# GpSimd's map additions moved behind the next image's statistics, and a later wait for the last special columns

## The reference

```python
def _gn(v, G=32, eps=1e-05):             # group norm, 12 channels a group
    g = v.reshape(B, H, W, G, C // G)
    m, s = mean and var of g over (1, 2, 4)
    return ((g - m) / sqrt(s + eps)).reshape(v.shape)

def conv(x, w1, b1, w2, b2, bias_w, bias_b):
    bias = x @ bias_w.T + bias_b
    xf = rfftn(x.reshape(B, H, W, 4, 96), axes=(1, 2), norm='ortho')
    xr, xi = xf.real, xf.imag            # below: einsum('...bd,bdk->...bk')
    r1 = relu(xr * w1[0] - xi * w1[1] + b1[0])
    i1 = relu(xr * w1[1] + xi * w1[0] + b1[1])
    r2 = r1 * w2[0] - i1 * w2[1] + b2[0]
    i2 = r2 * w2[1] + i1 * w2[0] + b2[1]
    return irfftn(complex(r2, i2), s=(H, W), norm='ortho') + bias

out = x + conv(_gn(x), ...)
```

## Time and profile before

| | us |
|---|---|
| median of three executions | 462.18 (461.31 to 462.39) |
| the profiled execution | 459.74 |
| its span in the profile | 457.6 |
| PE busy | 400.7 |
| DVE busy | 344.6 |
| ACT busy | 227.7 |
| POOL busy | 66.5 |

### The profile page before, as it was taken

The page is one execution under the profiler, slowest core; times in us unless marked ns, Lnnn a source line. Parts: engine busy times, 40 slices in busy tenths (PEclk is TensorE's granted clock), DMA queues, the critical chain, the costliest instruction groups (busy, mean ns, idle before and its releaser), DMA issues.

```text
span 457.6 us, 19262 instructions
## 1 busy us (share of the span) xinstructions
PE 400.7 (88%) x8530; PEld 355.4 (78%) x8530; DVE 344.6 (75%) x768; ACT 227.7 (50%) x504; POOL 66.5 (15%) x72
## 2 busy tenths in 40 slices
PE   4529778899899998999899998999899998995896
PEld 4418667787788988988788988988788887984794
DVE  3676988887797788868688788768787778769324
ACT  2632765326644476427643566437642575435320
POOL 0000007600060005100150006000240007000000
PEclk9758999999999999999999999999999999998899
DMA  6770000053001700052001700151002600130003
GB/s 212 212 210 0 4 1 4 2 184 130 3 5 36 278 4 4 26 178 112 4 4 50 265 4 4 35 208 73 5 3 94 221 3 4 37 140 1 4 4 138
DMA packets 12566, 33.22 MB, mean 73 GB/s; under 512 B 4994, under 2 KB 6692, under 8 KB 12484
## 3 DMA queue, kind: packets, MB, share of 16 engines
q1 hardware_dynamic: 12484, 32.00, 20.1%
HBM read 16.26 MB, written 12.58 MB: 63 GB/s over the span
## 4 chain that ended last, share of the span: by engine, by line
PE 62%; DVE 22%; issue 4%; SPq 4%; ACT 4%; DMA 2%; DVEq 0%
PE bank L552 62%; DVE r L1066 2%; DMA bias_all<-in_bias_b 2%; DVE rsum L1059 2%; DVE xs L1006 2%; DVE xs L1008 2%; DVE z L991 2%; DVE xs L1004 1%; DVE dev L1022 1%; DVE dev L1024 1%; SPq L511 1%; DVE sX L1020 1%; SPq L506 1%; DVE rho L991 1%; DVE g L1073 1%
## 5 line engine op out<-in xcount | busy, mean ns | idle before, releaser
L552 PE MATMUL bank<-biasw,y 128*64 128x384 f16 x1152 | 112.5, 339 | 4.5 <-DVE g L1073 4.4
L552 PEld LDWEIGHTS bank<-biasw,y 128*64 128x64 f16 x1152 | 94.2, 196 | 7.8 <-issue 5.2
L552 PE MATMUL bank<-w2s,rho 128*64 128x96 f16 x3072 | 83.9, 208 | 0.2 <-issue 0.2
L552 PEld LDWEIGHTS bank<-w2s,rho 128*64 128x64 f16 x3072 | 80.8, 109 | 3.6 <-issue 2.8
L907 ACT ACTIVATE z<-bank 128x384 f16<-128x384 f32 x72 | 35.2, 489 | 65.7 <-PE bank L552 65.0
L552 PE MATMUL bank<-w1R,y 128*128 128x192 f16 (+3 forms) x768 | 59.6, 228 | 1.6 <-issue 1.1
L552 PE MATMUL bank<-tab,x_sb 128*128 128x128 f32 x384 | 52.5, 290 | 9.6 <-DMA x_sb<-in_x 5.8
L991 DVE SCALAR_TENSOR_TENSOR z<-bank,z 128x384 f16<-128x384 f32 x72 | 40.0, 557 | 26.3 <-ACT z L907 25.9
L552 PEld LDWEIGHTS bank<-tab,x_sb 128*128 128x128 f32 x384 | 48.2, 201 | 14.3 <-issue 8.0
L892 ACT ACTIVATE g<-bank 128x384 f16<-128x384 f32 x64 | 31.0, 484 | 55.8 <-PE bank L552 55.7
L991 DVE SCALAR_TENSOR_TENSOR rho<-bank,rho 128x256 f16<-128x256 f32 (+2 forms) x128 | 40.1, 364 | 23.8 <-ACT rho L925 15.4
(11 more groups left out here) (104 smaller groups left out, 464.4 us busy)
## 6 DMA issues: line engine op xcount, KB each, us to landing
x_sb<-in_x SPq DMA_DIRECT2D x16, 768.0 KB, 6.8
out<-o_sb SPq DMA_DIRECT2D x14, 768.0 KB, 3.5
y<-y SPq DMA_DIRECT2D x24, 128.0 KB, 2.8
out<-o_sb SPq DMA_DIRECT2D x8, 192.0 KB, 1.9
tab<-in_tab SPq DMA_DIRECT2D x1, 672.0 KB, 5.8
o_sb<-in_bias_wt SPq DMA_DIRECT2D x4, 144.0 KB, 2.8
b1s<-in_b1h SPq DMA_DIRECT2D x1, 384.0 KB, 5.0
tab<-in_tab SPq DMA_DIRECT2D x1, 291.5 KB, 2.7
```

Source lines behind the costliest of these rows:

```text
L552: return nc.tensor.matmul(o, lhsT, rhs, start=start, stop=stop, **kw)
```

## The change

Three things are changed. The third bias product of `p4` stands before j = 7 and no longer before j = 6. The `gi` loop is entered when seven of eight banks of `rho` are evacuated; the wait for the eighth stands in `c2_rho` of gi = 0, between half 0 and half 1. GpSimd waits for all 23 steps of the statistics of image b + 1 (for the last image: those of image 7 again) and then does the map additions of image b itself.

```diff
@@ p4 @@
                 for j in range(8):
-                    if j in (2, 4, 6):
-                        gi = j // 2 - 1
+                    if j in (2, 4, 7):
+                        gi = {2: 0, 4: 1, 7: 2}[j]
                         if more:
                             c2_bias(b, p, gi, more, first)
                         elif gi:
@@ c2_rho @@
                 for half in range(2):
+                    if gi == 0 and half == 1:
+                        pe.wait_ge(rhoh_ready, 8 * b + 8)
+                        pe.wait_ge(rhol_ready, 8 * b + 8)
                     for slot, tile, k in ((0, 0, 0), (1, 1, 0), (2, 1, 1), (3, 2, 1)):
@@ image, on PE @@
                 p4(b, p, more, first)
-                pe.wait_ge(rhoh_ready, 8 * b + 8)
-                pe.wait_ge(rhol_ready, 8 * b + 8)
+                pe.wait_ge(rhoh_ready, 8 * b + 7)
+                pe.wait_ge(rhol_ready, 8 * b + 7)
                 for gi in range(8):
@@ GpSimd @@
             for b in range(BATCHES):
-                pool.wait_ge(rhol_ready, 8 * b + 8)
-                if b == 0:
-                    add_map(0)
-                if b + 1 < BATCHES:
-                    add_map(b + 1)
+                pool.wait_ge(dve_step, NSTEP * min(b + 2, BATCHES))
+                add_map(b)
```

## The result

The changed kernel takes 442.45 us (441.22 to 443.29), beside 461.88 for the kernel before on the same chip: a ratio of 0.9577, 95% interval 0.9551 to 0.9604. That is 19.4 us less. The prediction was 445.6 with a range of 443.0 to 452.0, so the sign and most of the size were right, and the time lies 0.55 us outside the range, on the fast side. Two later sessions on other chips gave 0.9604 (0.9575 to 0.9633) and 0.9629 (0.9596 to 0.9662).

A forecast was written before the change was run, and what follows sets the result against it. PE, busy for 88% of the span, was taken to set the pace. Image 0's 4.25, images 1 to 6's 11.3 and image 7's 1.05 sum to 16.6 us: 462.18 becomes 445.6, range 443.0 to 452.0.

The forecast's parts named there:

- Part 1: Start of gi = 0: later wait for bank 7 and moved bias product let half 0 start earlier, gaining 1.05 us an image.
- Part 2: Statistics without GpSimd end earlier; PE's waits at the first `g` (0.40 us) and before `variance` (0.44 us) go.
- The reading that others are not touched: On DVE, only instructions with two SBUF inputs wait for GpSimd's current addition; six statistics instructions an image lose 4.3 us.
- Image 7: Last image: only the gain at the start of gi = 0 counts, 1.05 us.
- Image 0: First image: waits of 2.0 and 1.2 us for `g` and `qv` go, plus 1.05 at gi = 0: 4.25 us.
- Part 3: GpSimd's additions, moved behind `scales`, meet the three `y_low`; DVE's idle time absorbs it, cost 0, at most 0.75 us an image.
- The first: At gi = 3 and `variance`, the squares, `g_high`, `g_low` chain is late instead: 451.4 us, chance 0.08.
- The second: Blocking moves to `y_low` and its full waits reach PE, 0.75 or 1.9 us an image: 451 to 459, chance 0.14.
- The third: At gi = 0 the new wait gains nothing, bank 6 being evacuated as late as bank 7 was: 454 us, chance 0.03.
- The fourth: At an image's tail `add_x` waits for GpSimd's additions, costing seven images 3.8 us each: slower, 472 us, chance 0.03.
- The fifth: Whole kernel: the change does not do what it says, no net change, chance 0.02.

The follow-up runs named there:

- GpSimd's part alone: Kernel before with only GpSimd's additions moved behind the statistics of the next image, TensorE as before: 451.85 us, ratio 0.980.
- without the reloads: Kernel before and changed kernel, each with the loads of images 2 to 7 left out: 459.34 and 439.97 us.
- the kernel with the additions in `c1`: Changed kernel with GpSimd's additions of image b at the start of c1(b), behind the last add_x of image b - 1: 445.38 us, ratio 0.9645.
- the late additions: Changed kernel with GpSimd's additions of image b only behind g_low 6, just ahead of add_x: 450.53 us, ratio 0.975.

## Why the prediction came close and was still wrong

**Part 1, 1.05 us an image: right.** Half 0 starts 1.32 us ahead of half 1, which starts where the whole started, and at the `mean` matmuls the lead is 1.02 us. The bias product covers bank 6; without it the wait for bank 6 is 0.6 us. What the prediction didn't say is that in images 0 to 6 this part is worth nothing alone; it put part 2 on top of part 1, where it should have said that part 1 stands on part 2.

**Part 2: right in mechanism, the step that failed in size.** The prediction took the gain at the first `g` and at `variance` as the recorded idle times, 0.40 and 0.44 us. By position they are more. From the start of the `c2_rho` of gi = 2 to the bias product of gi = 3 PE takes 1.62 us before (232.87 - 231.25) and 1.04 after (223.76 - 222.72), 0.58 less; from the next `c2_rho` to `variance` 1.65 (236.07 - 234.42) and 1.11 (226.41 - 225.30), 0.54 less. The idle time before a matmul is counted from the modelled end of the one before, and in a stream that does not wait the next one starts ahead of that end: 0.17 us ahead at the first place (222.72 + 1.21 - 223.76), 0.08 at the second (225.30 + 1.19 - 226.41). That much each wait cost beyond its row. The kernel with GpSimd's part alone, where these two waits go and nothing else, shows the same: 1.1 us an image (50.87 less 49.72 to 49.78), not 0.84. For an image both parts give 2.16 to 2.18 and not 1.89; over images 1 to 6 that is 1.6 us.

**The reading that others are not touched.** The prediction took only instructions with two SBUF inputs as held. A seventh statistics instruction, L1000, has one SBUF input and is held all the same, by 0.3 us each time but in the prologue, and L1042 by 0.8 in image 0, where GpSimd's second eight additions ran beside it. In the changed kernel both take 168 to 170 ns.

```profile
L1000 DVE TENSOR_SCALAR mc<-mc x8: 169/464/482, 15.5 to 380.7; 128x3 f32<-128x3 f32 x8
L1042 DVE TENSOR_SCALAR newton<-newton x8: 169/169/933, 22.4 to 390.5; 128x3 f32<-128x3 f32 x8
```

So one SBUF input is no safe sign in itself; it held for the reductions and for the SCALAR_TENSOR_TENSOR forms with a PSUM input. For the sum it makes no difference, as the statistics were early enough at both places either way.

**Image 7: 1.05 predicted, and right, though the two profiles differ by 1.9** (from the first `p4` bank behind the 3.37 us wait to the end: 457.6 - 422.69 = 34.91 against 440.8 - 407.76 = 33.04). A part is the clock. After that wait PE ran at the lower of its two levels for a while in both kernels, but for longer in the profile of the kernel before (columns: stretch, us, busy PE, PEld, DVE, ACT, POOL, PEclk, DMA share, GB/s), first before, then after:

```profile
422.00:424.00 2.00, 1.31 (x48) 1.33 (x48) 1.17 (x4) 0.49 (x2) 0.00 (x0) 0.50 0.00 0
424.00:427.00 3.00, 3.00 (x24) 1.89 (x18) 1.66 (x5) 1.07 (x3) 0.00 (x0) 0.50 0.03 8
```
```profile
407.00:409.00 2.00, 1.18 (x48) 1.12 (x48) 1.24 (x4) 0.76 (x3) 0.00 (x0) 0.80 0.00 0
409.00:412.00 3.00, 3.00 (x30) 1.97 (x26) 1.66 (x5) 0.88 (x2) 0.00 (x0) 0.57 0.03 8
```

A granted 0.50 is 1.2 GHz. The four banks and two products up to bank 7's end take 8.34 us before and 7.83 after, so 0.5 us are the clock's, and this varies from one execution to the next; it belongs to no edit. From bank 7's end on it is 26.57 against 25.21, 1.36 less, and 0.3 to 0.4 of that is a stall without a releaser that the kernel before has at 435.9. About 1.0 us is left for the edit.

**Image 0: 4.25 predicted.** 54.03 against 49.63 us from `p4` to `p4` is 4.40, and 4.67 when the unexplained stalls in it (0.88 and 1.15) are set aside. The same two waits are in it, so it is probably short for the same reason, by 0.4.

**The sum.** By the traces the edits give 4.7 + 6 x 2.16 + 1.0 = 18.7 us, where the prediction had 16.6, about 2 us too little. From the same 462.18 that would have been 443.5. The last 1.0 us down to 442.45 is no more than equal kernels differ by: the medians of the kernel before were 460.22 to 461.88 in four sessions, those of the changed kernel 442.45 to 443.29 in three. The differences of medians, 19.4, 18.0, 16.9 and, without the reloads, 19.4, lie around 18.7; none of them is sharp enough to confirm it to better than 1 us. Single profiles are no sharper. The first pair of spans differs by 16.8: 4.40 in image 0, 11.26 from there to image 7 (the changed kernel has longer stalls, 3.3 us in its list against 1.7), 1.87 in image 7, less 0.73 that the changed kernel comes later to image 0. That this is so close to the predicted 16.6 is chance. The pair without reloads differs by 18.1 in span, and there image 0 gives only 3.16, as the changed kernel ran part of its `p4` at the lower clock (granted 0.75 from 63 to 67 us). What is sharp is the period of the middle images, and it carries the reading of part 2.

**The range** was drawn from the terms of the sum alone. Its lower end left 2.6 us below the forecast, and the mis-sized waits took 2.0 of them, so the scatter of 1 us was enough to leave it. That the time came out on this side of the bound is in part luck: the median of the third session, 443.29, lies inside.

**Part 3: right.** `y_low` is blocked, GpSimd stretched to 10.7 us (about 11 predicted), and the idle time of DVE absorbs it. `y_low`'s mean of 1606 ns is below the 1.8 to 2.2 us given: only the first of the three waited more than half an addition, and the mean takes in the prologue's three, which met none. The Trainium skill's page "SBUF — State Buffer", section "Who interferes with whom", has VectorE instructions with two SBUF inputs and GpSimd instructions that read SBUF exclude each other; the trace agrees on both sides, `y_low` longer by 0.27 to 0.56 us, GpSimd's eight additions by 3.0 (10.7 against 7.7 where nothing stood in their way), `g_low` and `add_x` not.

**The rivals.** The first (another chain late at the same places) falls: no wait is left there. The second falls by the idle time before `add_x` and by the kernel with the additions in `c1`, whose middle images are no faster. The third falls by the timeline: half 0 starts at 218.73, before bank 7 is evacuated. The fourth falls by the late additions: `add_x` is at 617 ns beside GpSimd. The fifth falls by the result.

## What to carry to other kernels

Look at what an instruction's duration should be, not only at waits: an addition of three elements that takes 0.9 us is waiting inside itself, and no list of waits shows it. Removing a wait in front of a late engine is worth nothing until that engine is earlier; try such edits in pairs, and ask of each what the next wait is. Price a wait of TensorE from the start of one matmul to the start of the next, since the recorded idle time misses the part that lies under the last matmul's modelled end (0.08 to 0.17 us here). Before a small error of a forecast is explained, see how far the medians of equal kernels lie apart (up to 1.7 us here).

## What was not expected of the hardware

A VectorE instruction with two SBUF inputs was held for part of one GpSimd addition, never for two (`y_low` by at most 0.63 us, `r_low` by 0.80, L1045 in image 0 of the kernel before by 0.88, beside additions 0.96 us long), and GpSimd let it in between two of its own; with `y_low` between them the eight additions took 10.7 us, and 7.7 (387.17 to 394.86, those of image 7) when nothing stood in their way. A TENSOR_SCALAR on 128x3 float32 with a single SBUF input was held too (L1000, 169 to 464 ns).

PE had stalls of 0.2 to 2.3 us without a releaser at fixed places of the program. The longest were in the ninth unit of `c1`, where it runs through 48 matmuls in 0.7 us; there their size changed from execution to execution (0.88 to 2.25 us in image 0). One in image 2 was 0.52 us in both profiles of the kernel before and in all three of the changed one. Without the loads of images 2 to 7 they were gone behind image 0's `p4`, but for one of 0.41 us in image 7 of the kernel before.
